# A 32-slot ring for the gathered rows of a graph network, freed in quads of four slots

## The reference

```python
for l in range(3):
    agg = segment_sum(h[src], dst, num_segments=n)
    z = (1.0 + eps[l]) * h + agg
    h = relu(z @ W1[l] + b1[l]) @ W2[l] + b2[l]
x = layernorm(x + h)
hi, hj = x[src], x[dst]
e = leaky_relu(concat([hi, hj]) @ w, 0.2) @ a
exp_e = exp(e)
att = exp_e / segment_sum(exp_e, src)[src]
x = layernorm(x + segment_sum(hi * att, dst))
```

## Time and profile before

| what | value |
|---|---|
| median of 3 runs | 11765.27 us |
| the profiled execution, its own time | 11791.9 us |
| its span on the profile | 11790.1 us |
| POOL busy | 7314.1 us (62%) |
| PE busy, modelled | 5307.1 us (45%) |
| DVE busy | 4815.7 us (41%) |
| ACT busy | 1525.0 us (13%) |
| layer gathers, first to last start | 86.4 to 2543.8, 2613.0 to 5063.6, 5120.4 to 7563.7 us |
| score gathers, first to last start | 7704.9 to 10649.3 us |
| mean granted clock of TensorE | 0.636 |

### The profile page before, as it was taken

One profiled execution on the slowest core, in us unless ns is written; L12 is line 12 of the kernel. 1 busy time (PEld: TensorE's weight loads), 2 busy tenths in 40 slices (PEclk: granted clock), 3 DMA queues, 4 the chain that ended last, 5 costly groups with the idle time before them and its releaser, 6 DMA issues.

```text
span 11790.1 us, 134481 instructions
## 1 busy us (share of the span) xinstructions
PE 5307.1 (45%) x28366; PEld 4695.9 (40%) x28367; DVE 4815.7 (41%) x15058; ACT 1525.0 (13%) x4788; POOL 7314.1 (62%) x7786
## 2 busy tenths in 40 slices
PE   2333333343333333343333333465655655667886
PEld 2222222232222222232222232455555555556775
DVE  2222222232222222232222232454555555557888
ACT  0000000010000000000000000121211111216777
POOL 5666666656666666656666666555555555557886
PEclk7555555565555555565555555676777677778888
DMA  2111111121111111121111111244444445444444
GB/s 76 45 45 45 44 45 44 45 58 44 45 45 45 44 45 45 44 62 45 45 45 45 45 45 45 75 135 126 131 125 130 127 126 136 132 131 134 141 141 135
DMA packets 948880, 915.97 MB, mean 78 GB/s; under 512 B 268320, under 2 KB 785291, under 8 KB 948806
## 3 DMA queue, kind: packets, MB, share of 16 engines
q0 software_dynamic: 253760, 548.48, 17.9%
q1 hardware_dynamic: 629652, 264.39, 8.1%
q10 hardware_dynamic: 65426, 102.64, 3.1%
HBM read 769.30 MB, written 143.80 MB: 77 GB/s over the span
## 4 chain that ended last, share of the span: by engine, by line
another core or an unknown queue 43%; issue 18%; DVE 16%; PE 12%; DVEq 5%; POOL 4%; ACT 1%; DMA 1%; ACTq 0%; POOLq 0%; SPq 0%
DVE agg L1286 5%; PE psum L971 4%; POOL rows L635 4%; DVE agg L1274 4%; PE psum L1054 3%; DVEq L397 2%; PE psum L1072 2%; PE psum L1069 2%; DVE big L1504 2%; DVE work L1400 1%; DVE work L1393 1%; DVEq L1265 1%; DVE work L1390 1%; DVE hot L1257 1%
## 5 line engine op out<-in xcount | busy, mean ns | idle before, releaser
L971 PE MATMUL psum<-rows,hot 128*128 128x128 f32 x9984 | 2458.7, 422 | 4920.9 <-DVE agg L1286 3113.5
L635 POOL DMA_INDIRECT rows<-table_g,idx_now x3328 | 3143.2, 944 | 1876.7 <-issue 1069.1
L971 PEld LDWEIGHTS psum<-rows,hot 128*128 128x128 f32 x9984 | 2113.2, 309 | 5266.4 <-issue 4625.7
L1286 DVE TENSOR_TENSOR agg<-agg,psum 128x128 f32 x4992 | 1427.8, 286 | 5206.5 <-remote 4671.6
L635 POOL DMA_INDIRECT rows<-table_p,idx_now x1664 | 1622.0, 975 | 1334.7 <-SPq L511 855.4
L635 POOL DMA_INDIRECT rows<-in_x,idx_now x1664 | 1573.7, 946 | 884.9 <-issue 474.3
L1054 PE MATMUL psum<-work 128*128 128x98 f32 x3360 | 700.4, 377 | 968.8 <-issue 537.2
L1054 PEld LDWEIGHTS psum<-work 128*128 128x128 f32 x3360 | 637.9, 283 | 1029.5 <-issue 567.5
L1069 PE MATMUL psum<-big,work 128*128 x3328 | 854.6, 344 | 157.5 <-DVE work L1417 100.4
L1257 DVE TENSOR_TENSOR hot<-psum,exp_rel 128x512 f32<-128x512 f32 x1248 | 851.5, 682 | 0.2
L1072 PE MATMUL psum<-rows,ident 128*128 128x129 f32 x3328 | 810.8, 331 | 69.6 <-issue 61.4
(11 more groups left out here) (159 smaller groups left out, 4360.8 us busy)
## 6 DMA issues: line engine op xcount, KB each, us to landing
x_of<-rows SPq DMA_DIRECT2D x416, 256.0 KB
rows<-x_of SPq DMA_DIRECT2D x416, 256.0 KB
rows<-table_g,idx_now POOLq DMA_INDIRECT x3328
work<-rel_rows ACTq DMA_DIRECT2D x208, 256.0 KB
big<-lo_rows ACTq DMA_DIRECT2D x208, 192.0 KB
rows<-in_x,idx_now POOLq DMA_INDIRECT x1664
rows<-table_p,idx_now POOLq DMA_INDIRECT x1664
idx_now<-src_t SPq DMA_DIRECT2D x832, 4.0 KB
```

The lines of the kernel that those rows point to most:

```text
L635: pool.indirect_dma_start(out=slots[:, slot, 0:wide], out_offset=None, in_=table, in_offset=bass.IndirectOffsetOnAxis(ap=idx_now[:, at:at ...
L971: ins = pe.matmul(ps[q][:, (t % QUAD) * D:(t % QUAD + 1) * D], hot[:, t % HALF, :], row_of(t, D), start=True, stop=True)
L1286: dve.tensor_tensor(to, to, ps[q][:, (j % QUAD) * D:(j % QUAD + 1) * D], ALU.add).then_inc(added[j], 1)
```

## The change

The ring has 32 slots in the layers and in the score pass. In the layers the slots are 128 values wide, so 32 of them lie in the memory that held 16 wide ones. In the score pass the wide slots are spread in groups of four: four groups in `rows`, one in the memory of `hot`, three in `work`, for which `pos` and `den_hot` move to other places of `work`. Two neighbouring slots share one landing semaphore, which rises by 32 a lap of the ring. PE waits once for a pair of tiles and its loops are written out over 32 tiles. POOL waits for `free` before each quad, not each half. SP frees a quad two quads after it has issued that quad's store.

```diff
+RING = 2 * TPI
...
-        hot = sb("hot", [P, HALF, P], f32)
+        ring = rows[:, 0:RING * D].rearrange("p (t f) -> p t f", t=RING)
+        hot_mem = sb("hot", [P, QUAD * ROW], f32)
...
+        wide_mem = [rows[:, k * QUAD * ROW:(k + 1) * QUAD * ROW] for k in range(4)] + [hot_mem[:, :]] + \
+                   [work[:, wide_at + k * QUAD * ROW:wide_at + (k + 1) * QUAD * ROW] for k in range(3)]
...
-        USED = TPI
+        USED = RING
...
-            def release(group_turn, h):
-
-                sp.wait_ge(kept[h], 32 * (group_turn + 1))
+            def release(lap, q):
+
+                sp.wait_ge(kept[q % QUADS], 16 * (lap * (LAP // TPI) + q // QUADS + 2))
                 stand_alone(sp)
-                sp.wait_ge(rows_used, USED + LAYER_A * T + group_turn * TPI + (h + 1) * HALF)
+                sp.wait_ge(rows_used, USED + LAYER_A * T + lap * LAP + (q + 1) * QUAD)
                 sp.sem_inc(free, 1)
+            def keep_lap(lap, more):
+                for lane in range(AHEAD):
+                    for q in range(2 * lane, 2 * lane + 2):
+                        keep_quad(lap, q)
+                        if q % 2 == 1 and more:
+                            stage(lane, (lap + 1) * AHEAD + lane)
+                        release(lap, q - 2)
...
-                sp.sem_inc(free, 2)
+                sp.sem_inc(free, len(wide_quads) - 2)
...
-                            pool.wait_ge(free, i * AHEAD + lane + 1)
...
-                            if no != LAYER_A and j % QUAD == 0:
-                                pool.wait_ge(rows_used, USED - TPI + no * T + i * LAP + lane * HALF + j + QUAD)
+                            if j % QUAD == 0:
+                                if no == LAYER_A:
+                                    pool.wait_ge(free, i * (LAP // QUAD) + (lane * HALF + j) // QUAD + 1)
+                                else:
+                                    pool.wait_ge(rows_used, USED - RING + no * T + i * LAP + lane * HALF + j + QUAD)
...
-                        pe.wait_ge(row_in[t], gathers(no, i))
-                        ins = pe.matmul(ps[q][:, (t % QUAD) * D:(t % QUAD + 1) * D], hot[:, t % HALF, :], row_of(t, D), start=True, stop=True)
+                        if t % 2 == 0:
+                            pe.wait_ge(row_in[t // 2], pairs(no, i))
+                        ins = pe.matmul(ps[q][:, (t % QUAD) * D:(t % QUAD + 1) * D], hot[:, t % HALF, :], ring[:, t, :], start=True, stop=True)
```

More of the change, by code:

```diff
@@ L345, in gnn @@
         p_stored = sems("p_stored", 3)
-        kept = sems("kept", 2)
+        kept = sems("kept", QUADS)
         rel_in = sems("rel_in", 2)
@@ L433, in x_parts, with pairs @@
             return 2 if b == LAST else 1
-        def gathers(no, turn):
-            return 16 * (no * TURNS + turn + 1)
+        def pairs(no, lap):
+            return 32 * (no * (T // RING) + lap + 1)
         def laps(no, lap):
@@ L496, in stage_ahead, with keep_quad @@
                     stage(lane, lane)
-            def keep_half(turn, h):
-                for q in range(2 * h, 2 * h + 2):
-                    for j in range(q * QUAD, (q + 1) * QUAD):
-                        sp.wait_ge(row_in[j], gathers(LAYER_A, turn))
-                    sp.dma_start(x1_of[ds(turn * TPI + q * QUAD, QUAD), :, :].rearrange("r e d -> e r d"),
-                                 slots[:, q * QUAD:(q + 1) * QUAD, PW:ROW]).then_inc(kept[h], 16)
-            def release(group_turn, h):
-                sp.wait_ge(kept[h], 32 * (group_turn + 1))
+            def keep_quad(lap, q):
+                at = q % len(wide_quads)
+                for k in range(QUAD // 2):
+                    sp.wait_ge(row_in[(at * QUAD) // 2 + k], pairs(LAYER_A, lap * (LAP // RING) + q // len(wide_quads)))
+                sp.dma_start(x1_of[ds(lap * LAP + q * QUAD, QUAD), :, :].rearrange("r e d -> e r d"),
+                             wide_quads[at][:, :, PW:ROW]).then_inc(kept[q % QUADS], 16)
@@ L513, in stage_and_keep @@
             def stage_and_keep():
-                sp.sem_inc(free, 2)
+                for k in range(QUADS):
+                    sp.sem_inc(kept[k], 16)
+                sp.sem_inc(free, len(wide_quads) - 2)
                 with sp.Fori(0, LAPS - 1) as i:
-                    for lane in range(AHEAD):
-                        turn, h = i * (AHEAD // 2) + lane // 2, lane % 2
-                        keep_half(turn, h)
-                        stage(lane, (i + 1) * AHEAD + lane)
-                        release(turn, h)
@@ L522, in stage_and_keep @@
-                for lane in range(AHEAD):
-                    turn, h = (LAPS - 1) * (AHEAD // 2) + lane // 2, lane % 2
-                    keep_half(turn, h)
-                    if lane < AHEAD - 2:
-                        release(turn, h)
+                    keep_lap(i, True)
+                keep_lap(LAPS - 1, False)
             def store_g(stage_no, b):
@@ L560, in _ @@
             stage_and_keep()
-            for h in range(2):
-                sp.wait_ge(kept[h], 32 * TURNS)
+            for k in range(QUADS):
+                sp.wait_ge(kept[k], 16 * (TURNS + 1))
             sp.wait_ge(rows_used, USED + LAYER_B * T)
@@ L631, in gather @@
             def gather(lane, j, table, wide):
-                slot = (lane * HALF + j) % TPI
                 at = lane * HALF + j
-                pool.indirect_dma_start(out=slots[:, slot, 0:wide], out_offset=None, in_=table,
+                slot, landed = at % RING, row_in[at % RING // 2]
+                to = ring[:, slot, :] if wide == D else wide_quads[slot // QUAD][:, slot % QUAD, :]
+                pool.indirect_dma_start(out=to, out_offset=None, in_=table,
                                         in_offset=bass.IndirectOffsetOnAxis(ap=idx_now[:, at:at + 1], axis=0)) \
-                    .then_inc(row_in[slot], 16)
+                    .then_inc(landed, 16)
             def gather_rows(no, table, wide):
@@ L1070, in _ @@
                                       q_rows[:, ds(windows[t - h * HALF] * PW, PW)], start=True, stop=False)
-                            pe.wait_ge(row_in[t], gathers(LAYER_A, i))
-                            ins = pe.matmul(sums, ident[:, :], row_of(t, PW), start=False, stop=True)
+                            if k == 0:
+                                pe.wait_ge(row_in[u * PAIRS + j], pairs(LAYER_A, lap))
+                            ins = pe.matmul(sums, ident[:, :], wide_quads[(u * TPI + t) // QUAD][:, t % QUAD, 0:PW],
+                                            start=False, stop=True)
                         ins.then_inc(rows_used, 2)
                         if j in DEN_AFTER_PAIR:
-                            add_den(i, DEN_AFTER_PAIR[j])
+                            add_den(turn, DEN_AFTER_PAIR[j])
+            with pe.Fori(0, T // RING) as i:
+                for u in range(RING // TPI):
+                    score_turn(i, u)
             for q in range(QUADS):
```

30 lines of the change are left out of this document (18 added, 12 removed).

## The result

The changed kernel takes 11438.89 us, the median of 4 runs (11438.35 to 11444.09); beside it the kernel before takes 11754.13 us (4 runs, 11738.36 to 11786.93). The ratio is 0.973, 95% interval 0.9716 to 0.9744: 315 us faster. I had forecast 11640 us, 125 us under the 11765.27 us of the runs of before that I had then. The profiled execution took 11444.09 us, its span is 11442.2 us, 348 us under the span before.

The account below looks back on a forecast made before the run. PE's signals reaching other engines late while gathers follow each other bound the kernel. 11791.9 + 14 (layers) - 150 (score pass) = 11656 us profiled, times 0.9977 = 11629, given as 11640 us, range 11420 to 11880.

Parts of the forecast that it names:

- What bounds it: Layers and score pass: POOL's ring waits, 2062 us in all, come from PE's signals being seen late, not a short ring.
- The rule: PE's signals mostly stick during gathers, drain about 4 us after the last, pass freely until about 3 us into the next run.
- The layers: Layers: the cycle stays 16 gathers and 23.67 us with 32 slots; longer ends add 4.6 us a layer, +14 us for three.
- The last pass, cost nothing: Last pass, after the score pass: the change was costed at nothing.
- The score pass, number of standstills: Score pass: freeing by quads raises POOL's standstills from 1.5 to 1.7 or 2 a turn of 16 tiles.
- The score pass, price of one: Score pass: a standstill costs 3.93 + 0.8 - 1.26 = 3.5 us instead of 5.25; pass -220 or -115 us, taken as -150.
- the bounds of -480 to +250: Score pass: one standstill a turn would give -480 us, three would give +250 us.
- the sum (-136): Whole kernel: +14 us for the layers and -150 us for the score pass, from 11791.9 to 11656 us profiled.
- SP's releases, cost nothing: Score pass: SP makes 416 releases where it had 208, each two stores back; costed at nothing.
- Rival A: Layers and score pass: a longer ring covers late signals, -1207 and -430 us, some 10130 us as a median; chance 0.13.
- Rival B: Score pass: earlier restarts shut off signals, three standstills a turn, +250 us, some 12030 us as a median; chance 0.16.
- Rival C: Layers and score pass: DVE's and PE's mutual waits set the pace, not gathers; only +14 us, 11780 us median; chance 0.24.

Follow-up runs that it names:

- g1_layers8: The changed kernel with POOL allowed only 8 gathers ahead in the layers and 12 in the score pass: 12411.94 us, ratio 1.0469.

## Why the prediction was right and where it failed

- *What bounds it.* Right as far as it went: PE's signals reach the others late while gathers follow each other, and the ring waits of the earlier trace rows are the effect of that. The rule was not one of the kernel, as I called it. In four of nine batches the same kernel is at the level that has no late signal at all, and even in a held one signals are prompt at 1.49 us between gathers. What I called "stuck while gathers follow each other" fits a lead being worked off.
- *The layers.* Forecast: a cycle that stays, and +14 us for their ends. The ends came as +10.4 us between the stages, but from first to last gather the layers were 52 us shorter. The cycle didn't stay at 16 gathers; it became 20, 4 and 16. The claim that the ring's size isn't in the count held within 2% and not exactly: 8, 16 and 32 ahead gave 2447.5, 2455.3 and 2428.7 us, and on one chip 32 slots took 28 us off three layers.
- *The last pass, cost nothing.* It cost 25.4 us. I had priced the slots that are left to work off at the end of a layer, and not those at the end of the score pass. In the held traces the time after the last gather goes with how far POOL may be ahead there: 1160 to 1166 us with 32, 1150 and 1143 with 16, 1140 to 1141 in the kernel before. In the open ones it is 1140.3 and 1138.7 us.
- *The score pass, number of standstills.* Close: 2.04 gaps a turn, where I had 1.7 to 2. That is a kinder count than mine. The earlier trace rows count every wait for SP, 154 at 5.25 us, and the gaps over 2 us of the same pass are 133 at 6.06 us, both 7.8 us a turn. Counted as in the earlier trace rows the change has 255 waits, 2.45 a turn, at 551.4 / 255 - 0.3 = 1.86 us.
- *The score pass, price of one: the step that failed.* I set 3.93 + 0.8 - 1.26 = 3.5 us, taking the drain of 3.93 us that the earlier trace rows show after a run of 16 as fixed. It grows with the run. After runs of 12 and 4 it was 3.13 and 2.14 us, and the standstill 2.29 us over the gaps, or 1.86 us by the count of the earlier trace rows. With the right price my own sum reads 20.2 + 2.04 x 2.29 = 24.9 us a turn, against 25.1 measured and the 26.2 or 27.2 that I took, and 3.4 us x 104 = 354 us saved instead of 150. Shorter runs were the very effect of the edit, and the earlier trace rows could have warned me: where the lead had not built up yet, signals were prompt. From these two values I chose -150 us out of -115 to -220; the -331 us lies outside both and inside the bounds of -480 to +250. So the wait was the right one and its size was wrong. Of the 212 us between the sum (-136) and the spans (-348), 181 are the score pass and 56 the layers with their ends, and the last pass takes 25 back. The sum itself gives 11629 us; the 11640 that I gave has no reason in it.
- *SP's releases, cost nothing.* Borne out: in the open batch, where no signal is late, the score pass took 2109.5 us with twice as many releases and 2108.9 before.
- *Rival A*, that more slots cover late signals: fell. 32 slots by halves in a held batch: 1.0006. In an open batch POOL does run through as A saw it (9826 us, A had 10130), but the kernel before does so too.
- *Rival B*, three standstills a turn: fell at 2.04. The 434 gaps of `g1_layers8`, 4.2 a turn at 3.39 us, are no case of it: they come from the wait for the landing of the quad just issued, and PE's signals were prompt.
- *Rival C*, a chain of DVE and PE that keeps its pace whatever the gathers do: fell, by the score pass and by the open batches.

## What to carry to other kernels

Where an engine waits at a ring, ask what ends the wait before adding slots: in the score pass a ring twice as long gave nothing, and asking for its slots by fours instead of eights gave all. A finer grain with too few slots behind it can also tie the engine to its own last transfer, as in the 3565.5 us of `g1_layers8`. Price a stall from runs as long as those that the edit will leave, not from those it removes. And run the kernel before again in every batch: this one has two levels, 9.82 and 11.75 ms, and a change that is worth 2.7% on one is worth nothing on the other.

## What the runs showed of the hardware

- The same kernel on the same kind of chip took 9820 to 9834 us in four batches and 11711 to 11858 us in five, the result's among them, at granted clocks of 0.62 to 0.65 in both but for one run at 0.754 (9822.14 us) and the one of 10279.04 us. The gathers take 0.94 to 0.98 us on POOL in both. What differs is when the semaphore that PE raises changes: 0.013 us after the matmul, or up to 16 us. The landings of the layers' gathers are on record 2.3 us after their start where signals are held and 2.5 us where not.
- In the held condition PE's signals are late when gathers of 128 rows of 512 bytes follow each other every 1.25 or 1.34 us, and prompt at 1.49 us. They come through 3.7 to 5.2 us after the last gather of a run of 12 to 24. What makes a batch held, and what path the signals share with the gathers, isn't known. All runs have a profile's span and clock, so none tells whether recording has a part in it.
- The best kernel tried in a held batch was 16 ahead by quads in the score pass, 0.9668 (0.964 to 0.9696) against 0.973 (0.9716 to 0.9744) for the change; these are different batches, so of the two only the score passes on one chip (2567.3 and 2584.6 us) compare directly. In the open batch it cost 0.2%: 1.0018 (1.0009 to 1.0028).
